# Four token transposes per batch at other slots of a decoder layer on one core

## What is computed

```
x = x + mixer(layernorm(x))                # state-space mixer
x = x + attention(layernorm(x), ctx, ctx)  # 32 query heads, 8 key heads, against 512 context tokens
x = x + moe(layernorm(x))                  # shared expert + top 2 of 16 experts

mixer(x):  xn = rmsnorm(x) * w_norm
           z, xi, dt, B, C = split(xn @ W_in.T)          # 1024, 1024, 16, 256, 256 columns
           xi = silu(conv4(xi)); dt = softplus(dt + bias)
           y  = scan over the tokens (decay exp(dt*A), input dt*mean(xi)*B, read out with C)
           y  = (y @ W_h2i.T) * silu(z)
           return y @ W_out.T + x
```

## Time and profile before

| | |
|---|---|
| median of 3 runs | 1233.63 us (1233.13 to 1237.44) |
| profiled execution, own time | 1236.07 us |
| its span, first to last instruction | 1234.2 us |
| TensorE (PE) busy | 1175.1 us, 95% |
| VectorE (DVE) busy | 692.3 us, 56% |
| ScalarE (ACT) busy | 475.3 us, 39% |
| GpSimd (POOL) busy | 315.0 us, 26% |
| TensorE's mean granted clock | 0.993 of full |

### The profile page before, as it was taken

How to read it: one execution, slowest core, us unless ns; L and a number is a source line. 1 busy time by engine, 2 the same in 40 slices (tenths; PEclk the granted TensorE clock), 3 DMA queues, 4 the chain that set the end, 5 groups by cost and what they waited for, 6 DMA issues and landing times. The chain is left out here.

```text
span 1234.2 us, 31130 instructions
## 1 busy us (share of the span) xinstructions
PE 1175.1 (95%) x13185; PEld 581.7 (47%) x13186; DVE 692.3 (56%) x1146; ACT 475.3 (39%) x669; POOL 315.0 (26%) x458
## 2 busy tenths in 40 slices
PE   5999999999999999999999999999998999999996
PEld 3444434444445544445545554544543444444442
DVE  3823586756788565668575787878466222222220
ACT  3311224533555453555453455555621222222221
POOL 6012310321221220221031131111012444343443
PEclk9999999999999999999999999999999999999998
DMA  8320673104283201364400244100137565677640
GB/s 202 102 78 22 187 168 98 48 16 117 62 164 85 72 24 28 88 119 99 113 15 15 101 93 80 71 3 3 71 130 230 102 172 134 166 194 230 159 87 14
DMA packets 113057, 122.17 MB, mean 99 GB/s; under 512 B 18928, under 2 KB 78448, under 8 KB 112800
## 3 DMA queue, kind: packets, MB, share of 16 engines
q1 hardware_dynamic: 101968, 99.11, 29.9%
q0 software_dynamic: 10528, 21.12, 8.7%
q10 hardware_dynamic: 432, 0.08, 0.0%
HBM read 94.63 MB, written 28.97 MB: 100 GB/s over the span
## 5 line engine op out<-in xcount | busy, mean ns | idle before, releaser
L676 DVE TENSOR_REDUCE mx<-ps_m 128x2 f32<-128x1024 f32 x256 | 312.8, 1222 | 195.1 <-PE ps_m L1009 190.5
L879 ACT ACTIVATE prob<-ps_s 128x1024 f32<-128x1024 f32 x256 | 261.9, 1023 | 324.5 <-PE ps_s L1009 323.7
L1009 PE MATMUL acc<-xnT,wring 128*32 128x512 f32 x1888 | 249.0, 592 | 0.6 <-DVE first_z L612 0.6
L1823 PE MATMUL ps_gu<-ring,xgT 128*128 x376 | 178.6, 598 | 3.8 <-DVE xgT L1541 2.0
L1009 PE MATMUL ps_s<-q_stack,k_stack 99*32 99x512 bf16 x2048 | 161.5, 380 | 4.0 <-ACT prob L879 3.4
L1009 PE MATMUL ps_m<-k_stack,q_stack 96*32 96x512 bf16 x1952 | 153.1, 380 | 9.5 <-DVE mx L676 7.9
L1541 DVE COPY xgT<-ps_x 128x512 f32<-128x512 f32 x47 | 32.5, 691 | 209.1 <-PE ps_x L1795 209.1
L1194 PE MATMUL ps_o<-prob,values 128*32 128x128 f32 x4096 | 138.6, 273 | 0.0
L1194 PEld LDWEIGHTS ps_o<-prob,values 128*32 128x32 f32 x4096 | 116.2, 110 | 45.4 <-issue 39.9
L1009 PEld LDWEIGHTS ps_m<-k_stack,q_stack 96*32 96x32 bf16 x1952 | 55.3, 96 | 127.5 <-issue 73.0
L1499 POOL DMA_INDIRECT out<-y,dest x47 | 74.4, 1584 | 156.1 <-DMA out<-y,dest 131.4
(11 more groups left out here) (284 smaller groups left out, 1178.1 us busy)
## 6 DMA issues: line engine op xcount, KB each, us to landing
ring<-in_w_experts SPq DMA_DIRECT2D x96, 256.0 KB, 5.6
wring<-in_w_in SPq DMA_DIRECT2D x80, 256.0 KB, 4.1
q_stack<-part_rows SPq DMA_DIRECT2D x96, 128.0 KB, 4.3
wring<-in_w_out SPq DMA_DIRECT2D x32, 256.0 KB, 3.1
part_rows<-part SPq DMA_DIRECT2D x20, 384.0 KB, 4.4
xt<-in_x SPq DMA_DIRECT2D x16, 256.0 KB, 4.4
out<-x SPq DMA_DIRECT2D x4, 1024.0 KB, 5.2
k_stack<-part_rows SPq DMA_DIRECT2D x48, 64.0 KB, 2.5
```

What stands on the lines that cost most here:

```text
L676: nc.vector.tensor_reduce(mx[:, n % G, 2 * u:2 * u + 2], ps_m[:, :, :], AX.X, ALU.max).then_inc(s_max, 1)
L879: nc.scalar.activation(prob[:, slot % PROB, :, :], ps_s[:, :, :], ACT.Exp, scale=SCALE).then_inc(s_exp, 1)
L1009: ins = nc.tensor.matmul(dst[c:c + 32, :], stationary[:, c:c + 32], moving, start=start, stop=stop, tile_position=(0, c))
L1823: ins = nc.tensor.matmul(ps_gu[p][:, :], xgT[:, p, k * P:(k + 1) * P], weights(own)[:, k * 2 * F:(k + 1) * 2 * F], start=(k == 0), stop=(k ...
```

## The change

The step list `TURN_AT` gives the slots m at which the token blocks 0 to 3 of the next batch are transposed and evacuated. It is read by TensorE (`m in TURN_AT`, transposes, ahead of the first mixer half) and by VectorE (evacuation, behind the maxima and the addition to x1). Nothing else is changed.

```
-    TURN_AT = (50, 52, 58, 60)
+    TURN_AT = (42, 46, 62, 63)
```

## The result

The changed kernel takes 1243.01 us (median of 20 runs, 1237.52 to 1252.05), the kernel before 1235.14 in the same rounds (20 runs, 1232.83 to 1245.19): ratio **1.0062**, 95% interval 1.0048 to 1.0077, slower by 7.9 us of medians. Measured again later on another occasion it was 1243.69 against 1235.14, ratio 1.0077 (1.0052 to 1.0103). Forecast were +6.0 us and 1239.6, range 1234 to 1246. Of the 3.4 us between 1239.6 and 1243.01, 1.5 lie in the base: the forecast stands on the median of three runs, 1233.63, and the 20 runs of the kernel before have 1235.14. The profiled execution has 1241.89 us, span 1239.8, against 1236.07 and 1234.2.

What follows compares the result with a forecast made beforehand. TensorE, busy 95% of the span, was taken as the bound, its pauses set by VectorE's queue order. Batch 0 +1.4 us and batches 1 and 2 +4.6 gave +6.0 on 1233.63: 1239.6 us, range 1234 to 1246.

Steps and rivals of the forecast that it cites:

- removed, tiled batch: Old slots 50, 52, 58, 60 in batches 1 and 2: four steps of 0.70 us disappear, -2.80 us each batch.
- m = 42, gate behind the evacuation: Batches 1 and 2: maxima and new evacuation delay the gate that inner product 2 needs, +1.2 us.
- m = 46 in addition, wait for the keys' remainder: Second step waits until VectorE takes the keys' remainder; first output product +1.83 us in all, m = 42 included.
- boundary: m = 62 and 63, tiled batches: step 4 waits for evacuation 3, next step-size projection +3.26 us, before removals.
- tiled batch: Batches 1 and 2, net of removals: +0.4 us from the middle and +1.9 from the boundary, each batch.
- batch 0: First batch, net of removals: -0.2 us in the middle and +1.6 at the boundary, +1.4 together.
- stream end: Sum over three batches: +1.4 us for batch 0 and +4.6 for batches 1 and 2, together +6.0.
- +0.66 for the middle: Batch 0, m = 42 and 46: estimated delay of the output products' start, 0.61 and 0.05 us, before removals.
- Rival B: The chain plus a clock fall at one or two of three boundaries, +2 to +3 us each; 1243.5, chance 0.28.
- A: The chain of waits at middle and boundaries as summed, clock stays; +6.0 us, 1239.6, chance 0.42.
- Rival C: Part of the delay is given back in later waits, or a wait costs half; +2.5 us, 1236, chance 0.20.
- Rival D: Idle time at m = 62, 63 and in batch 0 really filled; gain up to 7.4 us, 1227 to 1232, chance 0.10.

Runs made afterwards that it cites:

- the added products: Kernel before plus three 512-column products, results overwritten, on TensorE in batch 0's gap at m = 40, bank claimed earlier, no step moved; ratio 0.9991.
- the kernel of the pauses: Kernel before with steps at 43, 46, 58, 63 (batch 0: 43, 46, 58, 60), evacuations reordered on VectorE; 1230.98 us against 1236.65, ratio 0.9957.
- that with the earlier load: The kernel of the pauses with each batch's first query stack load issued two slots earlier; 1228.32 us against 1235.14 for the kernel before, ratio 0.9948.

## Why the prediction was right, and where it was off

All shifts in us, the forecast beside what the profiles of the changed kernel show.

| step of the sum | forecast | measured |
|---|---|---|
| removed, tiled batch | -2.80 | -2.84 |
| m = 42, gate behind the evacuation | +1.2 | +1.23 (slot 16, +3.99, against slot 14, +2.76) |
| m = 46 in addition, wait for the keys' remainder | +0.63 | +0.69 (slot 20, +4.68) |
| boundary | +3.26 | +3.36 |
| tiled batch | +2.3 | +2.44, +2.44 (again: +2.44, +2.42) |
| batch 0 | +1.4 | +2.76 (again: +4.09) |
| stream end | +6.0 | +7.65 (again: +8.95) |
| median | +6.0 | +7.9 |

**Right.** The mechanism and each term of the tiled batches: two waits with releaser xnT at m = 63 and 0, forecast 2.3 and 0.8 us, found 2.18 and 0.62 in batch 1; 0.6 us for "rest", found 0.49; the old places 0.7 us shorter. That the order on VectorE decides, was argued in the forecast and is shown for the boundary by the kernel that keeps every slot and turns the order (+0.80). In the middle, one kernel changed slot and order together, so there the rows show the wait and no run turns the order alone. SP's load of x went out at 306.02, 5.2 us later than in the earlier trace rows, and nothing waits for it, as assumed.

**Off: batch 0.** The terms were worked out at full clock, with +0.66 for the middle and +2.4 at the boundary. The boundary is there: TensorE idles 1.48 and 0.78 us, and from the addition of the last block to the projection it takes 2.84 us (132.83 to 135.67), 2.73 forecast:

```profile
134.26 0.63 PE L1066 MATMUL ps_t<-ident,xt 128*128 128x128 f32 x4 [1.48 <-DVE xnT L588]
135.67 1.08 PE L1092 MATMUL acc<-xnT,wdt 128*32 128x128 f32 x32 [0.78 <-DVE xnT L588]
```

What was missing lies before it. Order of time on TensorE and stretches of the changed kernel:

```profile
99.15 0.39 PE L1007 MATMUL acc<-y_parts,wh2i 128*128 128x512 bf16 x1 [0.57 <-DVE xz L617]
99.38 0.92 PE L1023 MATMUL ps_t<-ident,keys 128*128 128x128 f32 x4
...
101.81 1.09 PE L1066 MATMUL ps_t<-ident,xt 128*128 128x128 f32 x4 [0.65 <-DVE rest L669]
```

```profile
94.00:98.00 4.00, 2.22 (x10) 0.98 (x10) 1.89 (x3) 1.19 (x2) 0.12 (x1) 1.00 0.26 64
98.00:100.00 2.00, 1.43 (x7) 0.92 (x8) 1.11 (x2) 0.60 (x1) 1.86 (x2) 0.88 0.01 3
100.00:108.00 8.00, 7.35 (x17) 3.43 (x16) 2.25 (x4) 1.68 (x3) 4.83 (x5) 0.60 0.12 49
```

A second fall of the clock, from about 99.5 to 106.3 us: the four transposes take 1.09 us, those of the kernel before at full clock 0.60. The first addition to x1 comes at 111.79 instead of 109.69, +2.10, where the terms give -0.34 (the outputs of the scan start at 87.29 instead of 87.63) + 0.66 - 0.44 = -0.12, so this fall costs 2.2 us if the 0.66 is right, which no profile without a fall shows; the table of batch 0 gives 2.8. The step that was mis-sized is thus the term of batch 0, for which the forecast took the clock of the kernel before. Less of it arrives at slot 0: of +4.17 at the first projection of batch 1, 0.95 are given back at the first query transposes (0.79 of idling before them in the earlier trace rows, none now) and 0.46 up to the first maxima scores, which waited 0.26 us for a load before and don't now.

**Rival B** (a fall of the clock at the boundaries) has the number nearest to the median, 1243.5 against 1243.01, but by another fall than the one it named. It was right that such falls come, as the kernel of the last two steps shows twice, and wrong in place and size for the profiles of the changed kernel: 0.85 us each at a tiled boundary, not 2 to 3, and 2.2 to 2.8 us in the middle of batch 0, which no rival named. A and B together carried the sign. The Trainium skill ("TensorE: Matmul & The Clock Gate", Part 4) has it that transposes don't engage the full clock and don't count as busy in the same way. Where the full clock is granted, transposes do run at it here, by the 0.60 against 1.09 us above. Whether they count as busy, the runs neither prove nor refute: the clock fell behind the gap with the transposes of m = 63 in one kernel and not in another with the same gap.

**Rival C** (given back later) is out for batches 1 and 2: +7.64 at slot 110, +7.65 at 255. In batch 0 1.4 us are given back, 0.6 more than forecast. **Rival D** (pauses really filled) is out for this change, and true for other slots: -3.8 us over the two tiled batches with the steps at 43, 46 behind the maxima scores, and 63 with its evacuation ahead.

**Left open.** Whether the moved steps make the second fall in batch 0 more likely. All four profiles with steps at 42 and 46 have a fall between 94 and 108 us, but so have the one with only the last two moved and the one with the added products and none moved. The mean clock of the runs (0.9915, with the middle steps alone 0.9925 and with the other order 0.9903, against 0.9935) points that way and doesn't settle it.

## What to carry to other kernels

A pause of one engine is a place for work only if the whole step fits: look where its second half, here an evacuation, comes to stand in the other engine's queue, and who waits there. Two steps in neighbouring slots that share one bank, each evacuated behind the slot's other work, were a chain of both engines here: +3.36 us at the boundary, where the step at 63 alone added 0.81 (62 alone was not run). Issue the evacuation ahead of the slot's other work. Turning the order in one queue decided here between +3.4 and +0.8 us at a boundary, and one slot's difference for block 0, with another half slot for block 1, between +1.9 and +0.2 us in the middle. Before a shift is laid to an edit, look where it first appears: in batch 0 up to 2.9 us of it stood ahead of everything that was moved.

## What the runs showed of the hardware

The length of one idling does not tell here whether TensorE's clock falls. Behind 2.17 or 2.18 us at m = 63 it stayed at 2.4 GHz at both tiled boundaries in both profiles of the changed kernel, and fell to 1.2 GHz for 3.4 us behind 2.17 us at both in the profile of the last two steps alone. Before the outputs of the scan it fell around 2.93 us in the kernel before and stayed up through 3.83 and 3.65 us in the kernel of the pauses and that with the earlier load. And it fell at 96 us of the kernel with the added products, though no single idle time of the 10 us before was longer than 1.2 us.

A fall of 6.8 us cost 2.8 us in batch 0 and one of 3.4 us cost 0.85 at a tiled boundary. Half the fall's length, 3.4 and 1.7 us, is an estimate of the most it can cost, if TensorE had work in all of it.

A comparison of profiles of this kernel is therefore good to 0.05 us in the tiled batches, where no fall lies in them, and no better than 3 us in batch 0, where GpSimd's first product of the scan waits for a load until 79.8 to 83.5 us and falls come or not.
